# One fixed tile for each expert and 64 by the table, with the first four experts' weights loaded during the first stage

## The reference

```python
tokens = jnp.einsum('bpi,hi->bph', patches, W) + b          # 128 x 64 tokens, + 128 class tokens
h = concat([cls, tokens]) * pos_embed
h = h + attn(layernorm(h))
# mixture of experts on layernorm(h): E = 16 experts, TOP_K = 2, D = 128, DH = 512
gate = softmax((h @ router_w + router_b) / TEMP)
vals, idx = top_k(gate, TOP_K)
ey = silu(h @ ew1[e] + eb1[e]) @ ew2[e] + eb2[e]            # for the two experts of each token
moe_out = sum_k vals_k * ey_k + SHARED_SCALE * (silu(h @ sw1 + sb1) @ sw2 + sb2)
ff_out = silu(layer_norm(moe_out) @ ff_w1 + ff_b1) @ ff_w2 + ff_b2
return x + moe_out + ff_out
```

## Time and profile before

| what | before |
|---|---|
| time, median of 3 runs | 933.02 us (931.93 to 935.03) |
| the profiled execution, own time | 935.13 us |
| its span, first to last instruction | 933.3 us |
| mean granted TensorE clock | 0.980 of full speed |
| PE busy | 875.3 us (94%) |
| DVE busy | 669.5 us (72%) |
| ACT busy | 596.8 us (64%) |
| POOL busy | 435.5 us (47%) |
| mean DMA rate | 200 GB/s |

### The profile page before, as it was taken

One profiled execution on the slowest core, in us unless ns is written; L12 is line 12 of the kernel. 1 busy time (PEld: TensorE's weight loads), 2 busy tenths in 40 slices (PEclk: granted clock), 3 DMA queues, 4 the chain that ended last, 5 costly groups with the idle time before them and its releaser, 6 DMA issues. The chain is left out here.

```text
span 933.3 us, 22329 instructions
## 1 busy us (share of the span) xinstructions
PE 875.3 (94%) x5920; PEld 796.6 (85%) x5920; DVE 669.5 (72%) x2240; ACT 596.8 (64%) x1064; POOL 435.5 (47%) x374
## 2 busy tenths in 40 slices
PE   2999999999999999998897999999999999799996
PEld 2788888888888888887786999999999998688885
DVE  8468888787888878885755777776777774766671
ACT  3466667677776676676854666666666665567774
POOL 7012445554555555552641555665665564333330
PEclk9899999999999999999987999999999999899999
DMA  9999999999999988664167788888888873133321
GB/s 221 220 208 221 233 248 245 250 254 251 248 253 236 235 232 221 167 199 150 59 165 236 220 246 254 246 249 253 246 253 248 234 213 119 48 101 101 101 87 44
DMA packets 193915, 186.96 MB, mean 200 GB/s; under 512 B 16413, under 2 KB 168314, under 8 KB 193626
## 3 DMA queue, kind: packets, MB, share of 16 engines
q1 hardware_dynamic: 182784, 166.24, 68.2%
q0 software_dynamic: 9376, 19.42, 6.4%
q10 hardware_dynamic: 1722, 0.93, 0.5%
HBM read 150.48 MB, written 36.04 MB: 200 GB/s over the span
## 5 line engine op out<-in xcount | busy, mean ns | idle before, releaser
L1426 PE MATMUL bank<-xf,wp 128*128 128x256 f32 x1280 | 310.4, 391 | 5.4 <-ACT xf L628 5.4
L1426 PEld LDWEIGHTS bank<-xf,wp 128*128 128x128 f32 x1280 | 235.5, 190 | 47.5 <-issue 4.1
L911 POOL DMA_INDIRECT y_tok<-region,dsti x160 | 164.1, 1026 | 133.2 <-DVE region L1249 97.9
L869 POOL TENSOR_TENSOR rstd<-var,neghalf 128x4 f32<-128x4 f32 (+2 forms) x51 | 76.3, 1496 | 270.5 <-DVE var L1022 140.3
L628 ACT ACTIVATE xf<-region 128x1024 f32<-128x1024 f32 x160 | 174.0, 1136 | 19.8 <-DVE region L942 19.8
L885 POOL DMA_INDIRECT z_rows<-z,posg x130 | 157.2, 1209 | 45.5 <-issue 44.9
L1625 PE MATMUL bank<-region 128*128 128x128 f32 x1280 | 157.2, 276 | 0.0
L1625 PEld LDWEIGHTS bank<-region 128*128 128x128 f32 x1280 | 151.4, 193 | 0.0
L792 ACT ACTIVATE region<-bank,cols 128x256 f32<-128x256 f32 x320 | 126.1, 476 | 22.3 <-PE bank L1614 21.4
L1614 PE MATMUL bank<-parts 128*128 128x256 f32 x960 | 136.0, 291 | 0.3 <-DVE parts L1268 0.2
L942 DVE COPY region<-region 32x1792 f32<-32x1792 f32 x96 | 105.9, 1103 | 42.2 <-ACT hT L648 20.1
(11 more groups left out here) (179 smaller groups left out, 1213.8 us busy)
## 6 DMA issues: line engine op xcount, KB each, us to landing
region<-in_x SPq DMA_DIRECT2D x384, 196.0 KB
region<-in_L_ffn_ew SPq DMA_DIRECT2D x160, 256.0 KB
region<-z_rows SPq DMA_DIRECT2D x80, 130.0 KB, 2.7
region<-y_tok SPq DMA_DIRECT2D x16, 512.0 KB, 5.3
out<-region SPq DMA_DIRECT2D x65, 64.0 KB
ht_dram<-hT SPq DMA_DIRECT2D x16, 256.0 KB, 7.0
r_dram<-rr SPq DMA_DIRECT2D x16, 256.0 KB, 6.9
region<-ht_dram SPq DMA_DIRECT2D x16, 256.0 KB, 6.0
```

The source lines that it names most:

```text
L869: pool.tensor_tensor(dst, var, neghalf[:, 0:var.shape[1]], ALU.pow).then_inc(ready, 1)
L911: pool.indirect_dma_start(y_tok, bass.IndirectOffsetOnAxis(dsti[n % 2][:, i:i + 1], 0), yout[n % 2][:, i], None).then_inc(y_free[n % 2], 16)
L1426: ins = pe.matmul(out_cols, wp[:, s], cols_in, start=s == 0, stop=s == MAIN - 1)
```

## The change

Each expert's first tile is now fixed: tile `j` below 16 belongs to expert `j` and begins at row `j * CAP`. The table gives out the other 64 (`DYN`): each expert has `nt - 1` of them and they begin 256 rows further on. DVE writes the fixed part of `ejb`, `ejc` and `rowj` in the set-up. The weights of tiles 0 to 3 no longer hang on the table. SP loads them in the first stage, when group 14's images have been copied, and the rows of tiles 0 to 3 have constant addresses. The tails of experts 0 to 3 have a semaphore of their own, `tails_first`, and SP waits for it and for the scatters alone before it loads these rows. It waits for the other tails, the table and the spare rows before its loop. DVE splits `w1` of tile 0 right behind the table and no longer behind the last piece of the filler. The number of tiles, their work and their order on PE stay.

```diff
+FIRST, DYN = 4, EXPERT_TILES - E
+SPARE_AT = E * CAP + EROWS
+ZROWS = SPARE_AT + SPARE_TILES * EROWS
...
-                       .then_inc(tails_zeroed, 16)
+                       .then_inc(tails_first if n < FIRST else tails_zeroed, 16)
...
             for i in range(HT_LOW):
                 load_ht(i)
+            for j in range(FIRST):
+                sp.dma_start(w1b[j], ew1[j]).then_inc(w1_loaded[j], 16)
+                sp.dma_start(w2b[j], ew2[j].rearrange("(c p) d -> p c d", p=P)).then_inc(w2_loaded[j], 16)
             one(stores, GROUPS - 3)
...
-            sp.wait_ge(tab_ready, 1)
-            expert_weights(0, 0)
-            rows = row_numbers(sp, rowj[0:1, 0:4])
-
-            sp.wait_ge(tails_zeroed, 16 * E)
+            sp.wait_ge(tails_first, 16 * FIRST)
             sp.wait_ge(z_free[0], 16 + 16 * TOPK + 16 * TOPK * GT * GROUPS // 2)
             sp.wait_ge(z_free[1], 16 + 16 * TOPK * GT * GROUPS // 2)
-            sp.wait_ge(spare_zeroed, 16 * (SPARE_TILES - 2))
-            expert_rows(0, 0, rows[0])
-            for j in range(1, 4):
-                expert_rows(j, j, rows[j])
-                expert_weights(j, j)
+            for j in range(FIRST):
+                sp.dma_start(zin[j], z_rows[j * CAP:j * CAP + EROWS].rearrange("(p h) d -> p h d", p=P))\
+                  .then_inc(zin_loaded[j], 16)
...
             sp.wait_ge(htl_ready, EARLY)
+            sp.wait_ge(tab_ready, 1)
+            sp.wait_ge(tails_zeroed, 16 * (E - FIRST))
+            sp.wait_ge(spare_zeroed, 16 * (SPARE_TILES - 2))
             with sp.Fori(1, 1 + GROUPS) as i:
...
+            link(dve.tensor_copy(ejb[:, 0:E], iota))
+            link(dve.tensor_copy(ejc[0:1, 0:E], iota[0:1]))
+            link(dve.tensor_copy(rowj[0:1, 0:E], cst[0:1, C_BASE:C_BASE + E]))
...
             tlink(dve.tensor_copy(nt[:, :], nti[:, :]))
+            tlink(dve.tensor_scalar(nt[:, :], nt[:, :], -1.0, 0.0, ALU.add, ALU.max))
...
-            tlink(dve.tensor_scalar(ejc[:, :], bank[TEJ_BANK][0:1, 0:EXPERT_TILES], float(E - 1), None, ALU.min))
-            dve.tensor_copy(rowj[:, :], bank[TEJ_BANK][0:1, P:P + EXPERT_TILES]).then_inc(tab_ready, 1)
+            tlink(dve.tensor_scalar(ejc[:, E:], bank[TEJ_BANK][0:1, 0:DYN], float(E - 1), None, ALU.min))
+            dve.tensor_scalar(rowj[:, E:], bank[TEJ_BANK][0:1, P:P + DYN], float(EROWS), None, ALU.add).then_inc(tab_ready, 1)
...
             dve.wait_ge(tab_ready, 1)
+            split_w1(0, 0, 0)
             for i in range(FILL, EARLY):
...
             sh_rows(EARLY - 1)
-            split_w1(0, 0, 0)
```

More of the change, by code:

```diff
@@ L271, in build @@
         nti = sb("nti", [P, E], I32)
-        ejd = sb("ejd", [P, EXPERT_TILES], BF16)
+        ejd = sb("ejd", [P, DYN], BF16)
         one_e = sb("one_e", [P, E])
@@ L498, in expert_weights, with expert_rows @@
                 ex = sp.value_load(ejc[0:1, bass.ds(j, 1)], min_val=0, max_val=E - 1)
-                sp.wait_ge(w1l_ready, j - 3) if n >= 4 else None
+                sp.wait_ge(w1l_ready, j - 3)
                 sp.dma_start(w1b[n % 4], ew1[bass.ds(ex, 1)].rearrange("o d h -> d (o h)")).then_inc(w1_loaded[n % 4], 16)
-                sp.wait_ge(down_done, j - 3) if n >= 4 else None
+                sp.wait_ge(down_done, j - 3)
                 sp.dma_start(w2b[n % 4], ew2[bass.ds(ex, 1)].rearrange("o (c p) d -> p (o c) d", p=P))\
                   .then_inc(w2_loaded[n % 4], 16)
-            def first_row(j):
-                return sp.value_load(rowj[0:1, bass.ds(j, 1)], min_val=0, max_val=ZROWS - EROWS)
-            def expert_rows(j, n, row=None):
-                row = first_row(j) if row is None else row
-                sp.wait_ge(dstf_ready, j - 3) if n >= 4 else None
+            def expert_rows(j, n):
+                row = sp.value_load(rowj[0:1, bass.ds(j, 1)], min_val=0, max_val=ZROWS - EROWS)
+                sp.wait_ge(dstf_ready, j - 3)
                 sp.dma_start(zin[n % 4], z_rows[bass.ds(row, EROWS)].rearrange("(p h) d -> p h d", p=P))\
@@ L872, in _ @@
             for u in range(2):
-                at = E * CAP + u * EROWS
+                at = SPARE_AT + u * EROWS
                 pool.dma_start(z_rows[at:at + EROWS].rearrange("(p h) d -> p h d", p=P), zsrc).then_inc(z_free[u], 16)
@@ L1208, in tlink, with split_w1 @@
                 dve.wait_ge(tab_step, n[0])
+            def split_w1(j, n, h):
+                dve.wait_ge(up_done, j * EC - EC) if n > 1 else None
+                dve.wait_ge(w1_loaded[n % 4], h * 16 + 16)
+                dve.tensor_copy(w1h[n % 2], w1b[n % 4]).then_inc(w1h_ready, 1)
+                dve.wait_ge(w1h_ready, j + 1)
+                dve.tensor_tensor(w1l[n % 2], w1b[n % 4], w1h[n % 2], ALU.subtract).then_inc(w1l_ready, 1)
             ebase = cst[:, C_BASE:C_BASE + E]
@@ L1250, in rows_out @@
                                   bc(bias.unsqueeze(1), [P, EH, D]), ALU.add).then_inc(yout_ready, 1)
-            def split_w1(j, n, h):
-                dve.wait_ge(up_done, j * EC - EC) if n > 1 else None
-                dve.wait_ge(w1_loaded[n % 4], h * 16 + 16)
-                dve.tensor_copy(w1h[n % 2], w1b[n % 4]).then_inc(w1h_ready, 1)
-                dve.wait_ge(w1h_ready, j + 1)
-                dve.tensor_tensor(w1l[n % 2], w1b[n % 4], w1h[n % 2], ALU.subtract).then_inc(w1l_ready, 1)
             def split_rows(j, n):
@@ L1589, in _ @@
             ins.then_inc(tej_done, 1)
-            pe.matmul(bank[7][:, 0:EXPERT_TILES], ones[:, :], ejd[:, :], start=True, stop=True).then_inc(ejb_done, 1)
+            pe.matmul(bank[7][:, 0:DYN], ones[:, :], ejd[:, :], start=True, stop=True).then_inc(ejb_done, 1)
             for i in range(FILL + 2, EARLY):
```

10 lines of the change are left out of this document (5 added, 5 removed).

## The result

| what | before | after |
|---|---|---|
| time, median | 931.74 us (6 runs, 930.64 to 935.03) | 922.10 us (6 runs, 921.40 to 926.53) |
| ratio after / before | | 0.9908, 95% interval 0.9888 to 0.9927 |
| profiled execution, own time | 935.13 us | 921.74 us |
| its span | 933.3 us | 919.9 us |
| mean granted TensorE clock | 0.980 | 0.990 |

The ratio is 8.6 us of 931.7. The two profiled executions differ by more, 13.4 us of span, so the first question is where those lie.

The account below looks back on a forecast made before the run. PE's work and stalls were taken to bound the kernel. 4.34 + 2.45 + 1.97 - 0.3 = 8.46 us off gave 926.7 from the profiled execution or 924.6 from the median; forecast 925.0, range 922.7 to 929.8.

Parts of the forecast that it names:

- Second stall: PE's 2.69 us wait for tile 4's rows and 1.65 us of half clock behind it both go: 4.34 us.
- First stall: PE's 2.90 us wait for tile 0's rows shortens; they are issued at 488.3 and `up(0)` starts 2.45 us sooner.
- the 0.2 that was allowed: Delay of DVE ahead of the filler from one small operation added to the table: about 0.2 us.
- the scatter lands as late: Rival, chance 0.25: the last scatter lands as before, `up(0)` comes only 0.4 us sooner, the clock falls; 928.3 us.
- 4.17 us behind the scatter: Issue of rows 0 if DMA engines take turns between queues: T = 488.4, with the scatter's instruction ending at 484.23.
- the 4.07 from the rows: Issue of rows 0 from profile rows: T = 488.3, midway between 485.9 and 490.7, the scatter's instruction ending at 484.23.
- The clock: Behind PE's shortened wait for tile 0's rows, the granted clock stays at 1.00 instead of 0.50: 1.97 us.
- The term for DVE's second split: At full clock DVE's second split and its rows come late for `up(1)`: a loss of 0.3 us.
- The early weights: First stage: eight 256 KB loads delay group 13's store by about 3.5 us, landing near 415, at no cost.
- the 7 us to spare: Room between group 13's store landing near 415 and ACT writing `hT` for group 14 at 422.31: 7 us.

Follow-up runs that it names:

- the other chip: The kernel before and the changed kernel, both unchanged, run together on another chip: 997.76 and 994.67 us, ratio 0.9963 for the changed kernel.
- one pair early: Changed kernel with only tile 0's weights loaded in the first stage, those of tiles 1 to 3 between the rows: 997.82 us, ratio 0.9901 to before.
- weights late, third run: Changed kernel with the four weight pairs loaded behind the table again and tile 0's split behind the filler: 994.03 us, ratio 0.9955 to before.

## Why the prediction was right

It gave 925.0 us with 922.7 to 929.8. The median is 922.1, and the ratio times 931.74 gives 923.2. The sum did better than the forecast: it took 8.46 us off 933.02, the kernel before's median at that time, and with more runs that median is 931.74, from which the same sum gives 923.3. Both predicted stalls went, and the terms came out near what was said. What the prediction says of their causes is shown in part: that SP's list held rows 4 back is shown on two chips, and that tile 0's weights held the scatter back is argued only.

**Second stall.** Predicted 2.69 + 1.65 = 4.34. In the first comparison it is part of the 6.37, which holds the clock behind the first stall too: 4.34 + 1.97 - 0.3 = 6.01 was predicted. On the other chip it stands alone with 4.48. Rows 4 went out 6.08 us behind rows 0 (6.3 was predicted) and were wanted 12.9 behind them (12.6 or later). They had 6.8 and 7.9 us in the two profiles of the changed kernel; the 6.3 that the prediction held to be enough weren't put to the test there, but one pair early got by with 5.8.

**First stall.** Predicted 2.45 sooner at `up(0)`, came 2.44, counted from the last row numbers. (By the table's transposes it is 2.93, but these come 0.49 later themselves.) Rows 0 went out 4.27 us behind the scatter's instruction and not 4.07, but the scatter ended 0.16 sooner behind the row numbers, so they are 2.38 us sooner where 2.42 was predicted. The table costs more than the 0.2 that was allowed: 0.49 up to PE's transposes. Its added operation takes 0.25 with its link, and the comparison behind it took 0.46 and not 0.23. The filler is late by 0.91 at `sh_up(9)` and by 0.94 at its end, not by 0.72, of which 0.42 lie behind the table (2.89 against 2.47): `ht_low(9)` comes 1.03 later behind the table (2.16 against 1.13), since the split keeps DVE for 1.12 ahead of it, and PE, busy with another piece at first, sees 0.42 of that. DVE's timeline of the kernel after:

```profile
474.78 0.43 DVE L1217 CAST parts<-region 128x512 fp32r<-128x512 f32 x1
475.24 0.73 DVE L1219 TENSOR_TENSOR parts<-region,parts 128x512 fp32r<-128x512 f32 x1
475.90 0.68 DVE L1039 TENSOR_TENSOR parts<-region,parts 128x512 fp32r<-128x512 f32 x1
```

And rows 0, landed at some 485.53 + 2.26 = 487.8 (an estimate with the landing time of the earlier trace rows), were there before the filler's end at 488.2, so PE didn't stand for them. The margin is 0.4 us: rows issued as late behind the scatter as before (6.49 instead of 4.27) would have brought back some 1.8 us of stall, which is the rival "the scatter lands as late". It lost by this one number. Whether tile 0's missing weights made the scatter land sooner was not tried alone, and the first tails' own semaphore is a second candidate; on the other chips SP's tails last longer than the scatter and hide both. The Trainium skill, "DMA: Bandwidth & Descriptors", section "Queues, rings and completion order", has the DMA engines take turns between queues, from which the prediction had 4.17 us behind the scatter. The trace has 4.27, which lies near that and near the 4.07 from the rows, and can't tell the two workings apart.

**The clock.** Predicted to stay at 1.00 behind the first stall, worth 1.97. It did. From `t_in(0)` to `up(0)` it took 1.90 us, where 1.95 was predicted, with 0.75 and 0.37 of idle time in it. But the argument for it was weak. It rested on one stall of 1.98 us that was followed by full clock, and left out two of the same trace, 2.02 us at 431.20 and 2.10 at 464.22, that were followed by 0.52 and 0.58. The runs have counterexamples to it at shorter waits: 1.58 us at 454.7 in the changed kernel's own profile (0.50 behind it), and 0.75 and 1.14 us in weights late, third run, where `up(0)` took 2.21 us and `up(1)` 2.57, in a stretch whose mean clock was 0.66 (527 to 532). Behind the changed kernel's 0.75 and 0.37 the clock held in all six profiles that have them (`up(0)` in 1.69 to 1.71), behind 0.75 and 1.14 in four of five. So the term came true, but it was no safe one. The term for DVE's second split was 0.3 and came as 0.1 (`up(1)` follows `up(0)` by 1.73, and the window from 490 to 495 has PE busy throughout).

**The early weights.** Eight loads kept SP for 6.4 us (403.98 to 410.40), not 3.5, one of them for 2.03. The store of group 13 so went out 6.6 us later. ACT's timeline of the kernel after has its writing of `hT` with the same short wait for PE as before:

```profile
422.41 0.78 ACT L648 ACTIVATE hT<-bank,cols 128x512 f32<-128x512 f32 x1 [0.68 <-PE bank L1434]
```

The DMA engines moved 350 GB/s there, more than the 321 that I had used, so the 7 us to spare held. In no profile is ACT's wait there for this store; it is the same 0.65 to 0.68 us for PE in all fourteen.

**What was luck.** Up to the last row numbers 2.81 us, and 0.99 in the third stage, are clock in the main, and lie outside the change. That the clock held behind `t_in(0)` is the luck inside it, by up to 1.97 us. The prediction took the profiled execution of before as 2.1 us over the median and left that out at the end, which was the right way to treat it: 13.4 us less in the profiles are 8.6 in the ratio.

## What to carry to other kernels

At a seam between two stages, write down for each transfer when it is issued, when it lands and when it is wanted. Here one list put 11.4 us between the rows of the first tile and those of the fifth, and the landing took 5.6 to 6.3 more, 17 to 18 in all, where PE would have wanted them after 14 to 15 (12.9 in the changed kernel). What lay between, constant weights and reads of a table, need not be at the seam. A stall of TensorE is worth more than its length when half clock follows it (2.7 us cost 4.3 here, twice), and a stall that is hidden on one chip by a delay ahead of it can be open on another, so look at the margins (0.4 us here) and not only at the stalls. And when you cut two traces at a common place, see that the change doesn't move the place itself: here the cut at the table hid 0.49 us of cost, and the cut at the last row numbers shows it.

## What the runs showed of the hardware

- The same stall of 2.02 us was followed by a granted clock of 0.52 in one execution and 1.00 in the other. The Trainium skill, "TensorE: Matmul & The Clock Gate", section "What's actually happening", has the window run freely; by that rule both can be, and the traces agree. Executions of the changed kernel on one chip lay at 921.4 to 922.3 (four) and 925.8 and 926.5 (two), with a mean clock of 0.988 to 0.994 and of 0.985 and 0.988.
- The same waits of 0.75 and 1.14 us ahead of `up(0)` were followed by full clock in four profiles and by half clock in a fifth.
- Chips differ, or what else goes on around them; no run tells these apart. On three others the kernel before took some 66 to 80 us more. PE was busy for 95% of 560 to 700 us instead of 100%, and for 94.47 of the 100 us from 75 on, in the first stage, instead of 99.62.
- On those chips ACT's four tail issues were followed by idle time named "remote", 8.0 to 10.6 us in all twelve profiles, which is what made the filler late. ACT's timeline of the changed kernel there:

```profile
505.06 2.17 ACTq L419 DMA_DIRECT2D z_rows<-zeros  x4
514.27 1.26 ACT L694 ACTIVATE xf<-bank,cols 128x512 f32<-128x512 f32 x2 [9.79 <-remote]
```

The kernel before has 9.76 there, so it isn't the change's. SP's twelve tails of 128 partitions took 13.9 to 15.4 us there against 10.0 to 10.2. What holds both engines was not found.
